# Splitting the bias add of the first four projection banks on GpSimd into a v half and an x2 half

## The reference

```python
xn = _layernorm(x, axis=-1)
# attn (a Hyena operator); its input is xn, called x here
h = _layernorm(x, gamma, beta)
proj = (h @ W_in + b_in).reshape(Bn, Tn, 3, Dn)      # v, x1, x2
y = v                                                 # (B, D, T)
y = _fft_conv(y, k0, Tn) * x1
y = _fft_conv(y, k1, Tn) * x2
attn = x + (y @ W_out + b_out)
# ffn with integer weights, scaled by 1/127
ffn = (silu(xn @ Wg.T) * (xn @ Wu.T)) @ Wd.T
```

## Time and profile before

| | us |
|---|---|
| median of 3 runs | 337.95 |
| lowest and highest run | 337.05, 338.35 |
| the profiled execution | 336.99 |
| its span in the trace | 335.2 |
| PE busy in the span | 304.5 |
| DVE busy | 259.4 |
| POOL busy | 213.1 |
| ACT busy | 178.9 |

### The profile page before, as it was taken

The page is one execution under the profiler, slowest core; times in us unless marked ns, Lnnn a source line. Parts: engine busy times, 40 slices in busy tenths (PEclk is TensorE's granted clock), DMA queues, the critical chain, the costliest instruction groups (busy, mean ns, idle before and its releaser), DMA issues.

```text
span 335.2 us, 11905 instructions
## 1 busy us (share of the span) xinstructions
PE 304.5 (91%) x4945; PEld 238.4 (71%) x4945; DVE 259.4 (77%) x533; ACT 178.9 (53%) x382; POOL 213.1 (64%) x293
## 2 busy tenths in 40 slices
PE   0379998987999999999999999999999999989993
PEld 0167877985767777787777877778777866558982
DVE  2779999975686777595776879788777777879994
ACT  2665677773344444445454445443545444479991
POOL 6679898185888887678776768868777662200000
PEclk9999999999999999999999999999999999999999
DMA  7992053059878778696787967878687788001345
GB/s 231 339 366 69 4 172 143 3 179 371 364 268 332 259 297 312 244 389 222 318 316 259 386 221 314 305 268 356 232 355 271 293 345 330 25 1 62 128 150 168
DMA packets 21506, 81.01 MB, mean 242 GB/s; under 512 B 1479, under 2 KB 12619, under 8 KB 13259
## 3 DMA queue, kind: packets, MB, share of 16 engines
q1 hardware_dynamic: 19458, 77.47, 62.2%
q0 software_dynamic: 1840, 2.36, 2.4%
q10 hardware_dynamic: 152, 0.40, 0.4%
HBM read 75.50 MB, written 4.72 MB: 239 GB/s over the span
## 4 chain that ended last, share of the span: by engine, by line
PE 54%; DVE 18%; ACT 9%; POOL 7%; issue 6%; DMA 2%; SPq 0%; POOLq 0%; DVEq 0%
PE bank_c L315 14%; PE bank_p L315 11%; PE bank_g L315 10%; PE bank_u L315 9%; PE bank_d L315 9%; ACT vx L793 4%; ACT vx L785 3%; DMA res<-in_L_attn_x 2%; DVE sgh L1011 2%; DVE stats L825 2%; DVE hhl L1016 2%; DVE xT L845 2%; DVE vx L866 1%; ACT hhl L720 1%; POOL vhl L1235 1%
## 5 line engine op out<-in xcount | busy, mean ns | idle before, releaser
L315 PE MATMUL bank_d<-wd,hhl 128*128 128x256 f16 x384 | 84.3, 271 | 0.3 <-DVE hhl L1016 0.2
L315 PEld LDWEIGHTS bank_p<-wq,xT 128*128 128x128 f16 x1536 | 69.8, 98 | 16.2 <-issue 1.4
L315 PE MATMUL bank_p<-wq,xT 128*128 128x64 f16 x1536 | 79.0, 193 | 0.0
L315 PE MATMUL bank_g<-xT,wgu 128*128 128x512 f16 x192 | 66.2, 378 | 0.8 <-ACT sgh L714 0.8
L315 PE MATMUL bank_u<-xT,wgu 128*128 128x512 f16 x192 | 66.2, 378 | 0.7 <-DVE sgh L1011 0.7
L315 PEld LDWEIGHTS bank_c<-ybuf,bands 128*128 128x128 f16 x1024 | 51.8, 96 | 19.0 <-issue 2.5
L315 PEld LDWEIGHTS bank_c<-vhl,bands 128*128 128x128 f16 x1024 | 49.1, 96 | 18.4 <-issue 3.0
L315 PE MATMUL bank_c<-ybuf,bands 128*128 128x64 f16 (+3 forms) x1024 | 60.3, 184 | 2.1 <-issue 1.7
L315 PE MATMUL bank_c<-vhl,bands 128*128 128x64 f16 (+3 forms) x1024 | 57.3, 184 | 2.1 <-POOL vhl L1235 1.1
L720 ACT CAST hhl<-sgh 128x512 f16<-128x512 f32 x48 | 29.7, 619 | 50.4 <-DVE sgh L1011 50.4
L1229 POOL TENSOR_TENSOR vx<-vx,bias 128x512 f32<-128x512 f32 x32 | 37.5, 1172 | 29.4 <-DVE vx L866 29.4
(11 more groups left out here) (193 smaller groups left out, 554.6 us busy)
## 6 DMA issues: line engine op xcount, KB each, us to landing
bands<-taps_seq SPq DMA_DIRECT2D x64, 1024.0 KB, 8.3
out<-res SPq DMA_DIRECT2D x8, 512.0 KB, 3.5
res<-in_L_attn_x SPq DMA_DIRECT2D x3, 1024.0 KB, 16.1
res<-in_L_attn_x SPq DMA_DIRECT2D x2, 512.0 KB, 6.1
bands<-in_L_attn_W_in SPq DMA_DIRECT2D x1, 768.0 KB, 6.2
bands<-in_L_ffn_w_gate POOLq DMA_DIRECT2D x1, 768.0 KB, 10.6
bands<-in_L_ffn_w_up POOLq DMA_DIRECT2D x1, 768.0 KB, 13.6
vx<-in_L_ffn_w_down POOLq DMA_DIRECT2D x1, 768.0 KB, 15.5
```

The source lines that it names most:

```text
L315: return nc.tensor.matmul(o, w, m, start=start, stop=stop, skip_group_check=True)
```

## The change

For the first four banks (range 0) GpSimd adds the bias in two instructions of 256 elements per partition: the v half (`add_half_bias(n, 0)`) at the old steps, which alone signals `vx_ready`, and the x2 half (`add_half_bias(n, 1)`), which signals the new semaphore `x2_ready`, at steps 22 and 26 for the banks 0 and 1, and between `gate_1` and the x1 bias of group 0 in the main stage for the banks 2 and 3. `gate_2` of group 0 waits for all four. The wait for the bias itself moves from `add_bias` to the first half. Later banks are as before. No other engine's instructions move.

```diff
+    ADD_X2 = (22, 26, 46, 46)
...
             def add_bias(n):
                 r, m = divmod(n, NPB)
-                if n == 0:
-                    pool.wait_ge(bias_ready, 2)
                 pool.wait_ge(proj_ev, n + 1)
...
+            def add_half_bias(n, i):
+
+                if n == 0 and i == 0:
+                    pool.wait_ge(bias_ready, 2)
+                pool.wait_ge(proj_ev, n + 1)
+                tile = vx[:, 0, i, :, PB * n:PB * (n + 1)]
+                row = bias[:, :]
+                off = bass.AP(row.tensor, row.offset + 2 * D * i, [row.ap[0], [1, CR], [0, PB]])
+                ins = nc.gpsimd.tensor_tensor(tile, tile, off, ALU.add)
+                if i == 0:
+                    ins.then_inc(vx_ready, 1)
+                else:
+                    ins.then_inc(x2_ready, 1)
...
                 if b in ADD_BIAS:
-                    add_bias(ADD_BIAS.index(b))
+                    add_half_bias(ADD_BIAS.index(b), 0)
+                for n in range(NPB):
+                    if ADD_X2[n] == b:
+                        add_half_bias(n, 1)
                 if b in SPLIT_V:
                     split_v(SPLIT_V.index(b))
...
             def gate_2(G, h):
                 r, g = divmod(G, 2)
                 pool.wait_ge(c_added, 4 * G + 2 + h + 1)
+                if G == 0:
+                    pool.wait_ge(x2_ready, NPB)
...
                 gate_1(G, 0)
                 gate_1(G, 1)
+                if G == 0:
+                    for n in range(NPB):
+                        if ADD_X2[n] >= LAST:
+                            add_half_bias(n, 1)
                 if G < NG - 1:
                     add_x1_bias(G + 1)
```

More of the change, by code:

```diff
@@ L208, in hyena_ffn_kernel @@
         flag_ready, sc_ready, unit_tp, unit_h, unit_l = sem("flag_ready"), sem("sc_ready"), sem("unit_tp"), sem("unit_h"), sem("unit_l")
+        x2_ready = sem("x2_ready")
         proj_mm, proj_ev, vx_ready, vh_ready, vl_ready = (
```

## The result

| | before | with the change |
|---|---|---|
| median of 20 runs, us | 337.17 | 335.58 |
| lowest and highest run | 336.35, 339.19 | 335.01, 337.75 |
| the profiled execution | 336.99 | 335.59 |
| its span | 335.2 | 333.8 |

The ratio of the times is 0.9954, with a 95% interval of 0.9939 to 0.9970: 1.55 us less, between 1.0 and 2.1. The interval leaves out 1, so the gain is real, if small. The forecast was 0.7 us less; its size was less than half of what came. That range was drawn around the first median of 337.95; with 20 runs the kernel before has 337.17.

The account below looks back on a forecast made before the run. TensorE has most of the chain; GpSimd costs time only where it holds VectorE's tiny operations. Terms: -0.7 (tiny runs), 0 (stage end), 0 (group 0), giving 337.2 us against the 337.95 median; own range 336.4 to 338.0, all cases 335.5 to 338.9.

Parts of the forecast that it names:

- the rival on TensorE's stop in group 0: Group 0: TensorE's 1.68 us stop before 79.00 might go with the stage's earlier arrival; 335.9 to 335.6 us, chance 12%.
- The length of a half add: GpSimd's 256-element bias add was taken as 0.67 us, like the split, with ends 0.54 and 0.73.
- h: Symbol for the length of a half add on GpSimd, taken as 0.67 us.
- The first tiny run: VectorE's tiny operations at steps 20 to 22, held by GpSimd: last one ends at 51.44 instead of 52.10, 0.66 us earlier.
- The sum: Whole forecast: -0.7 for the tiny runs, 0 for the stage end, 0 for group 0.
- The second tiny run: VectorE's L930 and L931, steps 24 to 26: meet GpSimd's two norms, ending at 55.59 instead of 56.34, 0.75 us earlier.
- From there to TensorE: Low half of block 24 ends TensorE's wait at 57.34, so 0.6 to 0.75 us arrive; 0.7 taken.
- The stage's end and group 0: Bank 3's earlier v half meets 1.4 us slack; group 0's two halves fit GpSimd's idle time, 0.9 us left; both nothing.
- The slower rival: Second tiny run: bank 1's x2 half holds L930, then the split holds L931 to 56.90; +0.6 us, 338.5 us, chance 8%.

Follow-up runs that it names:

- experiment 2: Changed kernel, but banks 0 and 1 get one full add as before, so only banks 2 and 3 are split; 337.13 us, ratio 1.0007.
- experiment 4: Kernel before, GpSimd untouched, with the four 3-column tensor-scalar operations of VectorE's step 21 each written as three one-column ones; 335.36 us, ratio 0.9945.
- experiment 6: Kernel before with one-column operations at step 21 and the four two-column products as tensor-scalar operations with a scalar from memory; 335.38 us, ratio 0.9945.
- experiment 7: Changed kernel with one-column operations at step 21 and the products as tensor-scalar operations with a scalar from memory; 335.29 us, ratio 0.9939.
- experiment 11: Changed kernel with only the third tiny run's two products (`fold_scale`, step 26) as tensor-scalar operations with a scalar from memory; 335.68 us, ratio 0.9955.
- experiment 1: Changed kernel with the x2 halves of banks 2 and 3 right behind their v halves (steps 34 and 37); 335.63 us, ratio 0.9958.
- experiment 3: Changed kernel with the x2 halves of banks 0 and 1 at once behind their v halves (steps 19 and 20); 335.99 us, ratio 0.9962.
- experiment 10: Kernel before with only the first operation of the first tiny run (L816) in single columns; 335.84 us, ratio 0.9965.
- experiment 9: Kernel before with only the second tiny run's two products (L930, L931) as tensor-scalar operations; 336.70 us, ratio 0.9992.
- experiment 5: Changed kernel with the x2 halves of banks 0 and 1 at steps 30 and 32 instead of 22 and 26; 335.62 us, ratio 0.9953.
- experiment 8: Changed kernel with x2 halves of banks 0 and 1 at steps 30 and 32, one-column operations at step 21, products as tensor-scalar; 335.65 us, ratio 0.9943.

## Why the prediction was right and where it was off

**Place and mechanism: right.** The gain comes over VectorE's tiny operations, the weight pairs and TensorE, as the chain before said. The experiments show it from both sides: with the hold as before the rest of the change is worth nothing (experiment 2), and with the hold taken away on VectorE the unchanged GpSimd is as fast (experiments 4 and 6, beside 7).

**The number: in the range by luck.** Only the rival on TensorE's stop in group 0 put cases as low as 335.5 to 335.9, and it did not come true; without it 335.58 us would lie outside. Of the 1.6 us between the forecast of 337.2 and the measured time about half is the larger gain, and 0.78 us are the first median of before, which lay that much above the one of 20 runs.

**The length of a half add: 0.62 to 0.63 us** on its own, inside 0.54 to 0.73 and a little below the 0.67 taken. 256 elements less save 0.44 us here. By the Trainium skill (GPSIMD Engine Reference, Elementwise — side-by-side cycle accounting), 2.6 cycles per element at 1.2 GHz, it was to be an estimated 0.55 and h 0.52; the measured 0.44 us are 2.1 such cycles per element.

**The first tiny run: mis-sized.** "L816, from 49.52 as before, ends at 49.69" and "L818 ... is held by the norm that ends at 50.20" came nearly as written: 49.78 and 50.23, with L816 starting 0.10 later. The step that failed is "L819 by the norm that ends at 50.74, and L923 by what stands there now, the x2 half of bank 0": the old L819, now L821, ran free, so the last operation met the second norm instead of the x2 half and ended at 50.80 instead of 51.44. The sum took every operation that comes beside a norm as held, as in the rows of before. But L819 started 0.07 us behind the start of a norm before and was held (0.50 us), and 0.08 us behind one now and was not (0.17); why is open. The term was 0.66 and measured 1.40 us.

**The second tiny run: mis-sized, as a consequence.** I had it meet the two norms and gain 0.75 in all. 1.4 us earlier it meets the power ahead of them, and that does not hold it. The low half of block 24 starts 5.85 us behind the start of the first run instead of 7.80: 1.95 us gained there, where the sum had 0.75. The rows of before had only a hint that the power holds less: two copies of VectorE (L859) took 0.28 and 0.29 us beside a power at 46.73 and 47.93, and 0.38 us beside a norm of GpSimd at 29.09. The sum did not ask what would be met if the gain was larger.

**From there to TensorE: not all of it arrives.** Of 1.95 us, 1.41 reach the first convolution. The third run, which the sum left out and which was free before, is held now and gives back 0.45 (experiment 11). The last 0.09 us fit a TensorE that no longer waits for the low half: its stop of 0.50 us at 57.34 is gone, and the low half ends at 55.89, ahead of the matmul that uses it (56.06). The sum passed the whole 0.7 on, which is only right as long as TensorE still waits for VectorE there.

**The stage's end and group 0: right.** Nothing was won by the earlier v half (experiments 1 and 2), and 0.85 us of idle time are left before the split of bank 5, where the prediction said 0.9. In part two errors cancel there: the two halves took 1.58 us instead of 1.34, the x1 bias 1.04 instead of 1.23. The stop of TensorE in group 0, 1.68 us, is 1.59; the rival on it had no part beyond these 0.09 us.

**The slower rival** did not occur: the x2 half of bank 1 runs from 55.49 to 56.12, when the second run is over. Its mechanism did, at the place behind it: the third run's two products took 0.35 and 0.49 us, held by a split and a norm, where they took 0.16 before, and that is 0.45 of the 1.95 us. The prediction did not look at that run.

## What to carry to other kernels

Where a chain of tiny VectorE operations runs beside GpSimd, compare each one's duration with the shortest of its kind and its end with the ends of GpSimd's instructions: an operation that ends 0.02 to 0.04 us behind one of them was held. Such a chain is better taken out of reach (one-column tensor-scalar operations here, 8 instructions more and as fast as the change, without a new semaphore) than aimed past GpSimd's instructions, since its time then hangs on what each operation happens to meet. The cure has a price of its own: three one-column operations took 0.28 us, one free operation on 3 columns 0.16. And a piece of work cut in two where one engine waits for it may pay in a quite different place from the one that the cut seems made for.

## What the runs showed of the hardware

- Held by a running GpSimd instruction: tensor-scalar operations on 3 columns (up to 0.98 us instead of 0.16) and tensor-tensor products of two SBUF columns (0.61 instead of 0.16). Not held beside the same instructions: tensor-scalar operations on one column, with a constant (three in 0.28 us) or with a scalar from memory (0.20 to 0.21 us). The Trainium skill (SBUF — State Buffer, Who interferes with whom) names two kinds that contend: two-port modes and two SBUF inputs. The products are of the second kind; that the operations on 3 columns ran in a two-port mode is not shown here.
- The same section of the Trainium skill has the pair of ports held for a whole instruction. For GpSimd's bias adds, norms and splits the trace agrees; for its power on 8 elements it does not: products that started in the last 0.4 us of a power of 1.67 us took 0.15 and 0.16 us (changed kernel, experiments 3, 4 and 10). No product started earlier in one, so how it is in the rest of a power stays open; a copy of VectorE at 46.73 us of the kernel before started 0.28 us into one and took 0.28 us.
- At the boundary of two GpSimd instructions it is open who goes first. An operation that starts 0.07 to 0.09 us behind the start of a norm was held in the kernel before (51.06, norm from 50.99), in experiment 2 (50.98, norm from 50.91) and in experiment 9 (51.22, norm from 51.13), and not in the changed kernel (50.27, norm from 50.19), in experiment 3 (50.97, norm from 50.89), in experiment 5 (50.14, norm from 50.06) and in experiments 1 and 10; the norm of the changed kernel took 0.58 and those of experiments 1, 3, 5 and 10 0.59 instead of 0.56. What decides it stays open. The operation took 0.50 or 0.51 us where it was held and 0.17 where it was not.
- The granted TensorE clock of the changed kernel's profile is 0.50 from 20 to 25 us (the 1.2 GHz level), behind 10 us in which the engine was busy for 4.28; the kernel before has 1.00 there, behind 4.36 us, and so have experiments 1 and 8, behind 4.27 and 4.13 us. The first tiny run of the changed kernel starts 0.10 us later than in the profile before, which is within the scatter of a (49.34 to 49.87), so a cost of the lower clock is not seen.
